# Making the low part of each gathered token tile on TensorE and ScalarE instead of VectorE, in a two-layer routed network

## What is computed

```
xn = layernorm(x)                              # 2048 tokens x 128
top_logits, idx = top_k(logits(xn), 2)         # 2 of 8 experts for each token
scores = softmax(top_logits)
for e in range(8):
    a, g = split(x_rep @ w1[e].T)              # 128 -> 2 x 352
    he = (silu(a) * g) @ w2[e].T               # 352 -> 128
    out = out + where(expert_ids == e, he, 0)
combined = (out * scores).reshape(2048, 2, 128).sum(axis=1)
```

## Time and profile before

| | |
|---|---|
| median of 3 runs | 472.01 us |
| time of the profiled execution itself | 475.62 us |
| its span, first to last instruction | 473.9 us |
| TensorE busy | 346.5 us (73%) |
| TensorE weight loads busy | 247.2 us (52%) |
| VectorE busy | 347.8 us (73%) |
| ScalarE busy | 261.5 us (55%) |
| GpSimd busy | 243.2 us (51%) |
| mean granted TensorE clock | 0.876 |

### The profile page before, as it was taken

How to read it: one execution, slowest core, us unless ns; L and a number is a source line. 1 busy time by engine, 2 the same in 40 slices (tenths; PEclk the granted TensorE clock), 3 DMA queues, 4 the chain that set the end, 5 groups by cost and what they waited for, 6 DMA issues and landing times.

```text
span 473.9 us, 5780 instructions
## 1 busy us (share of the span) xinstructions
PE 346.5 (73%) x1491; PEld 247.2 (52%) x1491; DVE 347.8 (73%) x615; ACT 261.5 (55%) x440; POOL 243.2 (51%) x254
## 2 busy tenths in 40 slices
PE   1846879667975987779506848977887887887883
PEld 0435659356854866668403524544554554554542
DVE  5679998897864866648169759908688688688674
ACT  1477654546458346374505675355856856856820
POOL 3475300704763676776800049005577877877850
PEclk9977675959997898998956975997999999999997
DMA  6374100100111112120160000004658658668574
GB/s 175 94 200 128 25 1 1 45 11 24 46 39 29 34 41 81 43 42 21 35 190 0 0 0 2 0 0 89 126 101 161 123 116 163 122 119 162 112 152 111
DMA packets 36213, 35.09 MB, mean 74 GB/s; under 512 B 12166, under 2 KB 30839, under 8 KB 36183
## 3 DMA queue, kind: packets, MB, share of 16 engines
q0 software_dynamic: 7104, 21.90, 22.7%
q1 hardware_dynamic: 29078, 12.84, 10.2%
HBM read 13.29 MB, written 4.65 MB: 38 GB/s over the span
## 4 chain that ended last, share of the span: by engine, by line
PE 35%; POOL 19%; DVE 19%; issue 13%; ACT 6%; DMA 3%; another core or an unknown queue 2%; DVEq 1%; SPq 0%; POOLq 0%; ACTq 0%
POOL state L568 10%; PE psum L1376 5%; POOL xn_tok L572 4%; PE psum L1349 4%; POOL g_hi L581 3%; PE psum L1365 3%; PE psum L1389 3%; PE psum L1443 3%; PE psum L292 3%; PE psum L293 2%; PE psum L294 2%; PE psum L1352 2%; PE psum L1355 2%; PE psum L1338 1%
## 5 line engine op out<-in xcount | busy, mean ns | idle before, releaser
L1212 DVE TENSOR_TENSOR_SCAN state<-dec,win_t 128x1024 f32<-128x1024 f32 x32 | 73.4, 2293 | 26.5 <-ACT dec L777 26.5
L568 POOL TENSOR_SCALAR state<-state,ssm_cb 128x1024 f32<-128x1024 f32 x32 | 49.7, 1553 | 48.0 <-DVE state L1212 45.0
L812 ACT ACTIVATE sil<-psum,vec_t 128x512 f32<-128x512 f32 x64 | 43.2, 687 | 48.3 <-PE psum L294 37.7
L509 POOL DMA_INDIRECT parts<-t_out,part x39 | 41.0, 1050 | 48.3 <-ACT t_out L726 41.9
L1498 PE MATMUL psum<-hid,g_w 128*128 128x512 f32 x128 | 62.1, 599 | 0.0
L1221 DVE TENSOR_TENSOR hid<-sil,psum 128x512 f32<-128x512 f32 x64 | 41.7, 676 | 12.9 <-ACT sil L812 10.9
L497 POOL DMA_INDIRECT x_tile<-normed,token x39 | 41.3, 1059 | 13.4 <-issue 10.7
L292 PE MATMUL psum<-xn_hi,g_hi 128*128 128x512 f32 x64 | 39.7, 620 | 11.3 <-ACT sil L812 11.3
L1094 DVE TENSOR_TENSOR t_hid<-t_sil,psum 128x352 f32<-128x352 f32 x39 | 20.3, 521 | 32.3 <-ACT t_sil L710 23.5
L717 ACT ACTIVATE t_hid_t<-psum 128x384 f32<-128x384 f32 x39 | 19.2, 492 | 38.9 <-PE psum L1365 25.3
L1376 PE MATMUL psum<-w_out,t_hid_t 128*128 x234 | 37.5, 300 | 2.2 <-ACT t_out L726 1.4
(11 more groups left out here) (308 smaller groups left out, 887.6 us busy)
## 6 DMA issues: line engine op xcount, KB each, us to landing
xn_tok<-state POOLq DMA_DIRECT2D x32, 512.0 KB, 4.5
e_raw<-in_L_ffn_w SPq DMA_DIRECT2D x16, 128.0 KB, 2.2
both<-parts SPq DMA_DIRECT2D x4, 512.0 KB, 5.6
e_raw<-in_L_ffn_w SPq DMA_DIRECT2D x8, 176.0 KB, 2.6
res<-in_L_attn_x SPq DMA_DIRECT2D x4, 256.0 KB, 3.8
normed<-rows SPq DMA_DIRECT2D x1, 1024.0 KB, 5.2
g_raw<-in_L_ffn_w SPq DMA_DIRECT2D x16, 64.0 KB, 2.3
g_w<-in_L_ffn_w SPq DMA_DIRECT2D x16, 64.0 KB, 2.2
```

The lines of the kernel that those rows point to most:

```text
L509: pool.indirect_dma_start(out=parts, out_offset=bass.IndirectOffsetOnAxis(ap=part[:, n:n + 1], axis=0), in_=t_out[n % ORING][:, :], in_off ...
L568: own(pool.tensor_scalar(state[k][:, :], state[k][:, :], ssm_cb[:, i * GPI + k // 2:i * GPI + k // 2 + 1], 0.0, ALU.mult, ALU.add))
L812: act.activation(sil[:, c % 2, :], ps[c % 2][:, :], ACT.Silu, bias=vec_t[:, V_B1 + c // NBLK:V_B1 + c // NBLK + 1]).then_inc(h_silu, 1)
L1212: dve.tensor_tensor_scan(state[k][:, :], dec[n % DECS][:, at_half], win_t[:, at_half], 0.0, ALU.mult, ALU.add).then_inc(scanned, 1)
```

## The change

A constant `minus`, the identity times -1 in float32r, is made on GpSimd ahead of the first `consts_ready`. VectorE's `split_x` goes. In its place TensorE multiplies `minus` with `xt_hi` and adds the product onto the transposed tile in the same PSUM bank (`take_high`, placed after `hidden(n)` and ahead of `turn_hidden(n-2)`), and ScalarE copies the bank into `xt_lo` (`copy_low`, placed after `copy_hidden(n-2)` and ahead of `weigh_out(n-3)`). `x_lo_ready` now comes from ScalarE.

```diff
         ident = sb("ident", [P, P])
+        minus = sb("minus", [P, P], F32R)
...
+        x_taken = sem("x_taken")
...
             own(pool.affine_select(out=ident[:, :], in_=ident[:, :], compare_op=ALU.not_equal, fill=1.0,
                                    base=0, pattern=[[-1, P]], channel_multiplier=1))
+            own(pool.tensor_scalar(minus[:, :], ident[:, :], -1.0, 0.0, ALU.mult, ALU.add))
             pool.nop().then_inc(consts_ready, 1)
...
+            def copy_low(n):
+
+                act.wait_ge(x_taken, n + 1)
+                act.activation(xt_lo[n % TRING][:, :], ps[X_BANK][:, 0:P], ACT.Copy).then_inc(x_lo_ready, 1)
+
...
                 if 0 <= n - 2 < NTILE:
                     copy_hidden(n - 2)
+                if n + 2 < NTILE:
+                    copy_low(n + 2)
                 if n >= 3:
                     weigh_out(n - 3)
...
-            def split_x(n):
-
-                dve.wait_ge(x_hi_ready, n + 1)
-                dve.tensor_tensor(xt_lo[n % TRING][:, :], ps[X_BANK][:, 0:P], xt_hi[n % TRING][:, :].bitcast(F32),
-                                  ALU.subtract).then_inc(x_lo_ready, 1)
-
...
                     gate(n - 1)
-                if n + 2 < NTILE:
-                    split_x(n + 2)
...
+            def take_high(n):
+
+                pe.wait_ge(x_hi_ready, n + 1)
+                pe.matmul(ps[X_BANK][:, 0:P], minus[:, :], xt_hi[n % TRING][:, :], start=False, stop=True,
+                          skip_group_check=True).then_inc(x_taken, 1)
+
...
                     hidden(n)
+                if n + 2 < NTILE:
+                    take_high(n + 2)
                 if 0 <= n - 2 < NTILE:
                     turn_hidden(n - 2)
```

## The result

The changed kernel takes 492.46 us median (491.29 to 494.11, 4 runs) against 472.05 us (471.5 to 473.81, 4 runs): ratio 1.0402, 95% interval 1.0355 to 1.0449. The forecast was 489.9 us, slower; the range 478 to 502 holds the result.

The account below looks back on a forecast made before the run. TensorE was read as fullest, VectorE's subtraction off the ordinary path. The 38 distances plus 1.4 us at the start gave a 146.4 us loop against 128.46, +17.9 on the 472.0 median: 489.9 us, range 478 to 502.

Parts of the forecast that it names:

- the product: `take_high` on TensorE, 128 columns: 0.13 us each, taken near a transpose's 0.11 us.
- the ordinary step: Loop over tiles, transpose to transpose through `turn_hidden`, `copy_hidden` and `copy_low`: 3.43 us against 2.64, 23 such steps, 78.9 us.
- the load uncovered behind the transpose's wait: `hidden`'s register load on TensorE, no longer done while `output` streams: 0.40 us more per ordinary step.
- The late low part: `x_lo_ready` from ScalarE comes too late for the next transpose: about 0.26 us more per ordinary step.
- the steps with groups: Steps where `copy_x` stands behind ScalarE's recurrence work: four sin at 4.53 us, 18.1; four double at 4.37, 17.5.
- The angles: Late angle work holds ScalarE 5.2 us: that step takes 7.7 us, the low-clock step behind it 4.8.
- the first four: First distances between `hidden` starts: two of 3.8 us, the third 4.8 at the low clock, then an ordinary 3.43.
- the base: The kernel before: loop 128.46 us, 26 of 38 distances 2.6 to 3.1 us; the difference was added to the 472.0 median.
- The covered load: Rival: `hidden`'s register load stays covered, ordinary step 3.03 us, result 480.7 us; chance 0.13.
- VectorE as the bound: Rival: `copy_low` lands before TensorE reaches the transpose, eight waits shrink, 3.4 us saved, 468.6 us; chance 0.04.
- The third rival: Loop clock falls and stays low: ordinary step 4.8 us, result 522, or 500 if one in three is hit; chance 0.10.
- So I leave the clock as it was: TensorE about 2.4 of 3.43 us busy in the ordinary step, above both compared stretches, so no clock change was forecast.

Follow-up runs that it names:

- both repairs of the low part's path: The changed kernel with `copy_low` ahead of `copy_hidden`, 481.82 us, ratio 1.0324; and the changed kernel with `hidden`'s register load ahead of the transpose's wait, 480.84 us, ratio 1.0321.

## Why the prediction was right, and where it was not

**Right: the ordinary step.** 3.43 us forecast, 3.33 to 3.37 measured. The largest term, the load uncovered behind the transpose's wait (0.40), was read from two kinds of steps of the kernel before: one in which the transpose waits and one in which it doesn't. What the prediction calls its reading is seen in the sequencer's records of those two steps; here is `hidden`'s load in the step that did not wait, then in the step that did:

```profile
L1331 PEldq TENSOR_LOAD <-tile_e x1: 298/298/298, 172.9 to 172.9; - x1
...
L1331 PEldq TENSOR_LOAD <-tile_e x1: 307/307/307, 167.3 to 167.3; - x1
```

The first starts at 172.88, 0.37 us ahead of the transpose and while `output` is still streaming (to 173.41); the second at 167.34, 0.02 us behind the transpose. `hidden` comes 0.85 and 0.86 us after the load's start. The run with `hidden`'s load ahead shows it by itself: transpose to `hidden` fell by 0.64 us, though the whole step only by 0.40: the second cost then came to light. The late low part (0.26) is the rest of a chain that is found link by link; no run isolates its size.

**Right: the steps with groups.** 18.1 + 17.5 = 35.6 us forecast for the eight, 36.9 measured. The two pairs at full clock took 4.43 and 4.45 us (forecast 4.53) and twice 4.29 (forecast 4.37); the rest of the difference lies in the two pairs that met the low clock. The angles were forecast at 7.7 + 4.8 = 12.5 us, measured 13.2. The loop without its start was forecast at 145.0 us and is 145.9.

**Right in the sum, not in its terms: the first four.** 3.8, 3.8, 4.8 and 3.43 were forecast, 15.8 together, and 3.50, 3.56, 4.58 and 4.73 measured, 16.4 together. The first two were put too long. The fourth was put far too short: I took it for an ordinary step, and it still ran at the low clock. The first `hidden` was forecast 1.4 us later and came 1.5 us later; 1.2 of that lie between the first transpose and it (6.3 us, before 5.1).

**Mis-sized: the product.** 0.13 us taken, 0.06 measured, half of the lower bound: the 0.11 us that a transpose takes is no floor for a product in a stream.

**Wrong as a sentence: "In an ordinary step `copy_x` is done at 174.34, well ahead of the end of `hidden`".** I took this for proof that the new wait is free there. The array indeed never waits there; the sequencer does: with the wait alone, the load behind it starts 0.05 us after the end of `copy_x`, 0.41 us before the array comes to `turn_hidden`. The wait alone costs 1.75%. In the changed kernel this cost is hidden behind the larger one: in the step above `output`'s load starts at 207.39, 0.60 us ahead of `turn_hidden`, and `output` follows `turn_hidden` after 0.33 us. The two costs overlap and don't add. That is why both repairs of the low part's path stopped at 2.91 us and not at 2.70; and it is luck, not insight, that the forecast came out with this cost missing.

**Wrong: the base.** "26 of 38 are 2.6 to 3.1 us, 12 are longer" was counted in a trace with waits of ScalarE on something outside the core; its loop is 8.4 us longer than that of the second trace. The forecast added 17.9 us to a median of 472; against the trace without these waits the change costs 145.7 - 120.0 = 25.7 us in the loop and 2.1 at its start. So the level was forecast well, but the size of the change only against the first measurement, where it was 20.4 us; against the later ones (26.7 us) it is a third too small. The sum for the changed loop hardly hangs on the disturbed steps: 146.4 less the second trace's 120.0, added to 465.75, gives 492.1, and 493.05 was measured. By parts, the 25.7 us are: the 22 ordinary distances 13.6, the eight with groups 7.0, the first four 3.5, the angles 1.6. Whether the waits were those of one profiled execution or of the whole first measurement isn't shown; that its four runs of the kernel before lie at 471.5 to 473.8 us, above all later ones (464.2 to 470.3), speaks for the latter. What the releaser was stays open.

**The rivals.** The covered load is refuted (0.87 us measured behind the wait, 0.23 with the load ahead). VectorE as the bound is refuted: freed of 7.4 us it only idles more. The third rival, a clock that falls in the loop and stays low, did not come about either: over ten steps of the changed kernel, two of them behind groups, it is 1.00.

```profile
122.00:158.00 36.00, 27.46 (x177) 23.07 (x177) 24.07 (x33) 19.66 (x56) 20.39 (x20) 1.00 0.14 38
```

Its ordinary steps have a gap of 0.6 us in 3.3.

**Too small: the time at the low clock.** The forecast had the start of the loop and the step behind the angles at the low clock and nothing else. What the trace shows of that clock, which the prediction gives as 1.2 GHz, is the record of 0.50 and the pace: from L1352 to L1355 behind the angles (155.50 to 156.09) two products of 352 columns take 0.59 us, 1.2 columns a ns; at 1.00 they take 0.32 us. "So I leave the clock as it was" held in the ordinary steps, but the low clock at the start lasted longer, and two pairs of steps with groups met it too. From 107 to 114 us, first the changed kernel, then the second trace of the kernel before:

```profile
107.00:114.00 7.00, 5.74 (x23) 5.08 (x23) 3.33 (x4) 1.95 (x6) 0.00 (x0) 0.50 0.00 0
...
107.00:114.00 7.00, 5.16 (x33) 4.21 (x32) 5.51 (x8) 5.94 (x15) 3.15 (x4) 1.00 0.07 21
```

Over the loop the mean is 0.90, against 0.93 in the second trace of the kernel before. The records have two levels only, 0.50 and 1.00, so that is about 29 us at 0.50 against 17 (an estimate: twice 0.10 x 145.7 and twice 0.07 x 120.0). At about half the pace (0.59 us against 0.32) 12 us more can account for at most 6 of the 27.8 us. What brings the spells about, and what they really cost, no run isolates.

**The expected signs.** The distance near 3.4 us, the 0.88 behind the transpose, the idle time of the product behind the groups and VectorE's added idle time are all there. The "some 30" waits of the transpose on `xt_lo` are not listed as such in the changed kernel (5 in the first trace); 31 are listed once both loads are ahead.

## What to carry to other kernels

That an engine is never seen idle at a wait doesn't make the wait free. Here TensorE's sequencer stood at it while the array still had 0.4 us of work ahead of it, and a register load behind it came late: the first product behind it came 0.85 to 0.90 us after the load's start in 28 of 34 steps. Issue register loads ahead of the waits of a step; here that alone made the kernel before 1.2% faster. But look also at which wait of the step before they now stand behind: in the changed kernel, with both loads at the top of the step, 2.0 to 2.2 us lie between a late product and the next transpose, where 1.2 did in a kernel that has no load at that place. Before work is moved to an engine with idle time, write down the chain that its result then hangs on in that engine's order, here `turn_hidden`, `copy_hidden`, `copy_low`, and compare it with the slack that the old place had.

## What I had not expected of the hardware

A product of 128 columns in a stream of float32r products took 0.06 us from start to start. A bare wait in TensorE's program, with a register load behind it, cost 0.12 us in each ordinary step, though it was already fulfilled when the array came to it, and 7.5 us in eight long ones, in which the array did stand at it (some low clock included). From the end of the copy that fulfils it to the first product behind the register load it mostly took 0.90 to 0.94 us, 0.05 of it up to the load's start, and 1.02 to 1.11 with the product in between.
